# Scatters spread over more turns and a fill between gathers, in a fused attention and mixture-of-experts layer

## The reference

```python
x = L0_attn_x
xn = _layernorm(x, axis=-1)
x = x + attn(xn, Wq, Wk, Wv, Wo, bo) + ffn(xn, router_w, router_bias, wg, wu, wd, swg, swu, swd)

# attention: 16 query heads of 16, one key and value head, rotation of half the
# head's columns, causal window of 64 tokens
scores = jnp.einsum('bhqd,bkd->bhqk', q, k[:, 0]) * scale + mask
out = jnp.einsum('bhqk,bkd->bhqd', softmax(scores), v[:, 0]);  return out @ Wo + bo

# experts: the best 4 of 64 for each token, gates normalised; two shared experts of width 256
_, topk_idx = jax.lax.top_k(logits + router_bias, K)
g = jax.nn.silu(jnp.einsum('nd,edf->nef', flat, wg));  u = jnp.einsum('nd,edf->nef', flat, wu)
routed = jnp.einsum('ne,nef,efd->nd', comb, g * u, wd)
shared = jnp.einsum('nsh,shd->nd', silu(flat @ swg) * (flat @ swu), swd)
return routed + shared
```

## Time and profile before

| | us |
|---|---|
| median of 3 runs | 372.5 |
| lowest and highest run | 371.52, 373.59 |
| span of the profiled execution | 407.3 |
| PE busy in it | 354.1 (87%) |
| DVE busy | 248.5 (61%) |
| POOL busy | 257.5 (63%) |
| ACT busy | 189.3 (46%) |

### The profile page before, as it was taken

One profiled execution on the slowest core, in us unless ns is written; L12 is line 12 of the kernel. 1 busy time (PEld: TensorE's weight loads), 2 busy tenths in 40 slices (PEclk: granted clock), 3 DMA queues, 4 the chain that ended last, 5 costly groups with the idle time before them and its releaser, 6 DMA issues.

```text
span 407.3 us, 8670 instructions
## 1 busy us (share of the span) xinstructions
PE 354.1 (87%) x2711; PEld 259.3 (64%) x2711; DVE 248.5 (61%) x717; ACT 189.3 (46%) x359; POOL 257.5 (63%) x522
## 2 busy tenths in 40 slices
PE   6698487988976899899999999999999997989753
PEld 3696355665654556448889999999974544545442
DVE  4668877877876878624554645454444419375676
ACT  3485667686766677533455555555532111010100
POOL 5677986777777665022446566877837757667560
PEclk9969989898999889957999999999999999999969
DMA  8940144444484446545988873577974324434341
GB/s 255 213 109 1 54 131 146 131 146 133 161 241 150 142 146 176 156 141 134 296 263 269 267 249 132 181 244 233 337 252 120 105 85 129 128 94 129 103 129 52
DMA packets 73037, 66.81 MB, mean 164 GB/s; under 512 B 9054, under 2 KB 68702, under 8 KB 72994
## 3 DMA queue, kind: packets, MB, share of 16 engines
q1 hardware_dynamic: 66433, 49.30, 40.8%
q0 software_dynamic: 6144, 16.79, 13.0%
q10 hardware_dynamic: 416, 0.18, 0.2%
HBM read 36.78 MB, written 29.23 MB: 162 GB/s over the span
## 4 chain that ended last, share of the span: by engine, by line
PE 64%; DVE 15%; another core or an unknown queue 8%; issue 5%; ACT 4%; DMA 2%; POOL 1%; SPq 0%; DVEq 0%; ACTq 0%; POOLq 0%
PE bank L650 14%; PE bank L675 8%; PE bank L589 8%; PE bank L515 5%; PE bank L624 4%; PE bank L540 4%; PE bank L609 4%; DVE xall L1092 3%; PE bank L436 3%; PE bank L491 3%; DVE xall L1324 3%; PE bank L417 3%; PE bank L523 2%; PE bank L458 1%
## 5 line engine op out<-in xcount | busy, mean ns | idle before, releaser
L1500 POOL DMA_INDIRECT xs_d<-spare,slot_i x64 | 64.2, 1003 | 29.3 <-PE bank L515 7.5
L1593 POOL DMA_INDIRECT wall<-y_d,y_row x64 | 61.4, 959 | 33.7 <-issue 18.3
L1519 POOL COPY spare<-wall 128x256 f32 x127 | 46.9, 400 | 29.9 <-PE bank L650 18.0
L650 PE MATMUL bank<-xall,spare 128*128 x508 | 64.1, 279 | 0.2
L1284 DVE TENSOR_TENSOR spare<-bank,spare 64x512 f32<-64x512 f32 (+1 forms) x64 | 44.1, 690 | 31.0 <-ACT spare L896 30.1
L650 PEld LDWEIGHTS bank<-xall,spare 128*128 128x128 f32 x508 | 59.4, 192 | 2.8 <-issue 0.7
L589 PE MATMUL bank<-xnT,xall 128*128 128x512 f32 x128 | 57.7, 594 | 0.5 <-issue 0.5
L908 ACT ACTIVATE spare<-bank 128x512 f32<-128x512 f32 (+1 forms) x62 | 33.7, 593 | 29.5 <-PE bank L675 17.9
L847 ACT ACTIVATE xall<-bank 98x1024 bf16<-98x1024 bf16 x32 | 32.7, 1021 | 22.6 <-PE bank L436 14.5
L855 ACT ACTIVATE xall<-bank 128x512 f32<-128x512 f32 x64 | 36.6, 601 | 12.5 <-PE bank L491 7.4
L609 PE MATMUL bank<-xall 128*128 128x256 f32 x128 | 32.0, 400 | 11.6 <-DVE xall L1309 8.3
(11 more groups left out here) (172 smaller groups left out, 656.0 us busy)
## 6 DMA issues: line engine op xcount, KB each, us to landing
y_d<-spare SPq DMA_DIRECT2D x31, 512.0 KB, 4.1
wall<-in_wg SPq DMA_DIRECT2D x16, 256.0 KB, 4.8
wall<-in_wu SPq DMA_DIRECT2D x16, 256.0 KB, 5.0
wdn<-in_wd SPq DMA_DIRECT2D x16, 256.0 KB, 4.5
spare<-xs_d SPq DMA_DIRECT2D x32, 128.0 KB, 2.8
small<-xs_d SPq DMA_DIRECT2D x32, 128.0 KB, 3.3
wall<-in_x SPq DMA_DIRECT2D x4, 512.0 KB, 5.7
base_d<-spare SPq DMA_DIRECT2D x16, 128.0 KB
```

The costliest lines, as they stand in the source:

```text
L650: ins = pe.matmul(up_bank_of(G)[:, j * P:(j + 1) * P], wcur[i % NW][:, c * 2 * F:(c + 1) * 2 * F], x_half[c][:, bass.ds(o, P)], start=c == ...
L1500: pool.indirect_dma_start(out=xs_d, out_offset=bass.IndirectOffsetOnAxis(ap=slot_i[:, T, k:k + 1], axis=0), in_=x_n[b][:, t, :], in_offset ...
L1519: pool.tensor_copy(wcur[i % NW].rearrange("p (c g f) -> p c g f", c=NC, g=2), wall[:, bass.ds(o, WE)].rearrange("p (g c f) -> p c g f", c= ...
L1593: pool.indirect_dma_start(out=yk[:, T, k, :], out_offset=None, in_=of, in_offset=bass.IndirectOffsetOnAxis(ap=y_row[:, T, k:k + 1], axis=0 ...
```

## The change

It has two parts, both on POOL.

**Scatters.** `SCATTERED_AT` becomes 4 in turns 0 to 11, 5 in turns 12 and 13, and 6 in turn 14, again 64 in all. Turn 0, which had none, does four, and between them the bias is added to the four tiles of the third sequence (`add_bias(2)`), which used to be done ahead of all scatters. The fourth sequence (`add_bias(3)`) is added in turns 12 and 13, after scatters 0 and 4. The fifth and the sixth scatter of a turn wait for the second `weighted` of that turn (`min(i, 4)`). In turns 1 to 11 each of the four scatters is followed by one rotation instruction.

**Fill.** After the gathers of each tile but the last, POOL fills the first 256 columns of `sg` with zeros, 15 times. The first fill waits for the end of stage 3 (`h`), each other for the fill before it.

```diff
-    SCATTERED_AT = lambda T: 5 if T <= 11 else 4
+    SCATTERED_AT = lambda T: 6 if T == NT - 2 else 5 if NT - 5 < T < NT - 2 else 4
@@
                 pool.tensor_tensor(x_in[b][:, t, :], x_in[b][:, t, :], bo_sb, ALU.add).then_inc(s["x_bo"], 1)
+                yield
+
+        def add_bias_whole(b):
+            for _ in add_bias(b):
+                pass
...
-        for b in range(1, B):
-            add_bias(b)
+        add_bias_whole(1)
         slots = scatter()
         for T in range(NT):
 
-            pieces = rotate(T + TPB) if 0 < T < NT - TPB else iter(())
-            if T:
+            if T == 0:
+                pieces = add_bias(2)
+                for i in range(SCATTERED_AT(T)):
+                    next(slots)
+                    next(pieces)
+            else:
+                if T < NT - TPB:
+                    pieces = rotate(T + TPB)
+                elif T == NT - TPB:
+                    pieces = add_bias(B - 1)
                 for i in range(SCATTERED_AT(T)):
                     if i < 2:
                         pool.wait_ge(s["by_query"], PER_T * T + 2 * i + 2)
                     elif i == 2:
                         pool.wait_ge(s["by_key"], PER_T * (T - 1) + 3)
                     else:
-                        pool.wait_ge(s["weighted"], QB * (T - 1) + i - 2)
+                        pool.wait_ge(s["weighted"], QB * (T - 1) + min(i, 4) - 2)
                     next(slots, None)
-                    next(pieces, None)
+                    if T < NT - TPB or i in (0, 4):
+                        next(pieces, None)
@@
+        def apart():
+
+            if not apart_n[0]:
+                pool.wait_ge(s["h"], NGRP)
+            else:
+                pool.wait_ge(s["apart"], apart_n[0])
+            pool.memset(sg[:, 0:D], 0.0).then_inc(s["apart"], 1)
+            apart_n[0] += 1
+
+        apart_n = [0]
@@
             for k in range(TOPK - 1 if T < FETCH_FIRST else TOPK):
                 fetch(T, k, y_d)
+            if T < NT - 1:
+                apart()
```

More of the change, by code:

```diff
@@ L117 @@
     "q_left diag wslice shifted gate k_out k_near o_out max mpart max_out rden a_tok ah hs h y_out_dve gT_dve expert_read with_x based sum "
-    "v_fill fill prep roped k_split weights down_weights x_bo "
+    "v_fill apart fill prep roped k_split weights down_weights x_bo "
 ).split() + [f"fetched{T}" for T in range(NT - 1)] + [f"last_fetched{k}" for k in range(TOPK)]
@@ L1550, in rotate_whole @@
                 pass
-        add_bias(0)
+        add_bias_whole(0)
         rotate_whole(0)
```

## The result

| | runs | median, us | ratio to before, 95% |
|---|---|---|---|
| before | 4 | 372.75 (371.52 to 373.59) | |
| after | 4 | 377.42 (377.03 to 378.86) | 1.0119 (1.008 to 1.0158) |

The change cost 4.7 us. The forecast was 377.1. That number is right and an important part of its reasoning is wrong, as the experiments show: the late semaphore updates that filled the profile of before are no matter of profiling. They are there, in runs too, on two of the three chips that were tried later, and on those the scatters' half of the same change is a gain. That the runs of before and after came from a chip without late updates is luck, as far as the forecast's sign goes. In the experiments the ratios leave out, for both kernels, the runs that lie well above that kernel's fastest; the medians are of all runs.

The account below looks back on a forecast made before the run. The PE held 64% of the chain of waits; 32.6 us of late semaphore updates were taken as mostly the profile's own. 372.5 us + 3.1 (later `picks`) + 1.5 (fills) = 377.1 us, 8-in-10 range 363 to 381.

Parts of the forecast that it names:

- I take the lateness as mostly the profiled execution's own: Attention and stage 4: late PE semaphore updates, 32.6 us of the chain, taken as mostly absent from runs without a profile.
- Part 1, turns 0 to 11, cost 0: Attention, turns 0 to 11: moved scatters and bias additions add no POOL work, so 0 us in the runs.
- rival 1: Late updates, attention and stage 4, occur in runs; removed: faster, 362 to 370.5 us (half size 366); chance 0.32.
- The tail, +3.1 us: End of attention: the last scatters land later, `picks` is issued later, and the whole 3.1 us delays the PE.
- the 3 to 4 foreseen: Last tile's scores: the PE would be idle 3 to 4 us before its first L491, instead of 0.90.
- Turns 12 to 14, 0 in the runs: Attention, turns 12 to 14: neighbouring fourth and fifth scatters add 1 to 2 us each in the profile, 0 in runs.
- Part 2, +1.5 us: Stage 4: 15 fills of 0.34 us delay POOL's gathers by 5.1 us; after slack, 1.5 us reaches the end.
- the bound of 14.5 us: Stage 4: the most the fills could gain if the lateness is real and they break it, 14.5 us.
- The sum: Whole kernel: 372.5 us plus 3.1 for later `picks` and 1.5 for the fills gives 377.1 us.
- The profile was to be 10 to 18 us shorter: Whole profile: the new span 10 to 18 us under 407.3, if neighbouring transfers cause the late updates.

Follow-up runs that it names:

- before again: The kernel before, unchanged, run and profiled again on a chip without late updates: 373.9 us, with a profiled span of 371.0 us.
- the profile whose clock stayed up: Profile of the kernel before with only the 15 fills added, on a chip without late updates: 374.7 us, ratio 1.0026.

## Why the prediction was right, and where it was not

**"I take the lateness as mostly the profiled execution's own": wrong.** On chips B and C the runs of before take 399 to 419 us themselves, and each span agrees with its own run. The step that failed is the one from span against median to "the profiled execution's own": it compared two chips. The rule that I cited beside it (the Trainium skill, "Runtime: NRT & Kernel Launch", "The launch sequence": a profile's total about 6.2 us over the reported time) did not bear on it. The span here runs from the first to the last instruction, and in every execution it lies 1.3 to 1.4 us under the time of its own run, so 34.8 us over was no property of profiling. My test ("if the span falls by over 10 us and the runs rise, the lateness was the profile's") came out as asked, and led astray in the same way: after was profiled on a chip without late updates. Only running before again showed it.

**Part 1, turns 0 to 11, cost 0: right** on a chip without lateness (the kernel with four scatters in turn 0 and an early end was faster than before, and turns 4 to 12 take 67.2 us in after and 67.3 in before again). On the others the scatters' half gains 2.0% (0.9801) in spite of the tail, and rival 1 holds there for this half. For the whole change the six runs on chip B have a median 4 us under before's, without a clear sign; rival 1 at half size was 6.6 us.

**The tail, +3.1 us: the right place, and its size by errors that cancel.** The landing of 3.1 us fits the 3.2 taken, but the last scatter starts 4.4 us behind turn 14's first L515 and not 3.5 (168.8 less 165.26): POOL was still in an earlier scatter when the two weighings ended. So `picks` moved by 3.9 us. The sum let its landing stay at 3.6 us and carried the whole shift onto the path; it took 1.7 us, and the PE's idle time grew by 2.1 us only (0.71 to 2.84), to just below the 3 to 4 foreseen. What was missing is what an idle PE costs afterwards: the clock at half for some microseconds, 0.6 us more than in before again, and 2.2 us more than in the profile whose clock stayed up. That makes 2.7 to 4.6 us by the profiles, and 2.2 us (1.0 to 3.4) by the timed runs of this half. By the figures of the Trainium skill (section "Anatomy of one DMA — SWDGE (gpsimd) path" of "DMA: Bandwidth & Descriptors") such a transfer takes an estimated 2.3 us. Here it is 3.1 us from the start of the last scatter to the issue of `picks`, and 2.2 us from the end of its 0.96 us on POOL, so whether the figure fits hangs on where it counts from.

**Turns 12 to 14, 0 in the runs:** nearly right on chip A. From the start of turn 12 to turn 14's first L515 it takes 19.3 us in after and 18.8 in before again.

**Part 2, +1.5 us: right, by two errors.** The 0.34 us of a fill came out as 0.19 on the path. The last gather starts 1.9 us later, counted from the first (372.32 less 289.54, 82.8 us, in after; 365.26 less 284.38, 80.9, in before again), and not 5.1 us: 15 times 0.19 is 2.9, and the gathers themselves take 61.9 us in all instead of 62.8. But the slack was also smaller: 1.4 us of the 1.9 reach the end, where I had given the gathers 1.4 to 2.6 us of slack. That fills would break the lateness of stage 4 (the bound of 14.5 us, which by its own terms, 407.3 less 392.6, should read 14.7) is refuted on chip C.

**The sum.** Between the profiles of before again and after, the parts that the change touches add up to 2.7 + 0.5 + 1.4 = 4.6 us, and the runs say 4.7. The two spans differ by 6.5 us; 2.3 us of that lie ahead of turn 4 (68.9 against 71.2), and the fills alone, with before's order there, has 71.3, so they are no cost of the change. My 3.1 + 1.5 meets the 4.7 since a shift of `picks` that I took too small, a landing that I took too long and a low clock that I left out nearly cancel.

**The profile was to be 10 to 18 us shorter; it was 29.8.** Before again has a span of 371.0, 36.3 us less with nothing changed, and after is 6.5 us above that.

Left open: why on two chips the PE's semaphore updates come late while POOL issues indirect transfers, and whether that belongs to the chip or to the session; what in stage 4 would prevent it, since fills do not; and why `picks` lands sooner when it is issued later.

## What to carry to other kernels

When a profile's span and the timed runs differ by far more than a microsecond or two, run the same kernel again for a second profile before any reasoning on "what profiling adds": here it was another chip, and the sign of the scatters' half depended on it. A wait that left TensorE idle for 2.84 us in a busy stretch had to be priced twice, once for itself and once for the low clock behind it (2.2 us); and the kernel before has to be looked at for the same cost, since it may pay part of it already. Where a queue of small transfers gates a later load, look at when the last of them is issued: ending the 64 scatters in turn 12 and not in turn 14 was worth 5.7 us on a chip without late updates. And before a term is carried through a load's landing, see whether the landing stays the same when the issue moves; here it fell from 3.6 to 1.7 us.

## What was not expected of the hardware

- Chips 8% apart on the same kernel (medians of 372 to 375 us against 406 to 407). On the slower ones the PE's updates come up to 9.3 us late where POOL issues indirect transfers, as in the earlier trace rows, those of the other engines never do, and in stage 3 none does; stage 3 is as fast (from the first L650 to the first gather 117.5 us in after on chip A, 173.72 to 291.51, 117.8, on chip B).
- On these chips an instruction of 0.33 us or more between two scatters, at four scatters a turn, brings the turns of the attention back to their length on chip A (38.4 us for turns 4 to 8 instead of 43.4 to 46.0). With more scatters in a turn and a POOL that never pauses it does not (37.6 us for turns 9 to 12, where chip A has 28.7), and a fill after each fourth gather took none of the lateness away in stage 4.
- PE idle for 2.84 us between busy stretches: granted clock 1.00 before, about 0.5 from within that time until 5.4 us behind it. An idle time of 0.7 us was followed by the low clock in one profile and not in another. With such a wait filled by 22 throwaway matmuls the clock stayed at 1.00, in two profiles.
- A load of 32 KB took 3.4 to 3.6 us to land when it was issued 3.3 to 3.7 us behind turn 14's first L515, and 1.7 us when it was issued 4 us later. The cause is not shown.
- A fill between two indirect gathers costs 0.19 us of its 0.33: the gap ahead of the next gather shrinks from 0.30 to 0.17.
